# Two-layer cross-attention and Mamba kernel on one core: all five instruction orders rewritten, PSUM banks dealt anew

## The chip, the cores and the metric

The kernel runs on one core of one Trainium2 chip. The metric is the device time of one execution in microseconds. The core has a matrix engine (TensorE, PE in the profile), a vector engine (VectorE, DVE), a scalar engine (ScalarE, ACT), GpSimd (POOL) and a queue that only issues transfers (SyncE, SP). Each engine runs its own instruction list in order and meets the others through semaphores.

## The reference

64 batches of 128 rows and 256 columns (`x`) pass two layers; `ctx` is the other input of both. Cut to its operations:

```python
# layer 0: attention with 16 heads of 16, relu on q, k, v
q = relu(x @ Wq + bq); k = relu(ctx @ Wk + bk); v = relu(ctx @ Wv + bv)
s = where(mask, (q . k) / 4, 1e-9); o = softmax(s) @ v
x = layernorm(o + x) * gamma + beta
# layer 1: a Mamba-2 block, then attention with 8 heads of 32
zxbcdt = rms(x) @ in_proj_w            # z 512, xBC 768, dt 8
xBC = silu(conv4(xBC)); dt = softplus(dt + dt_bias); decay = exp(-dt * exp(A_log))
h = h * decay + (dt * xh) (x) B;  y = h . C + D_skip * xh      # over the 128 rows
x = x + rms(y * silu(z)) @ out_proj_w
q = layernorm(x) @ Wq; k = ctx @ Wk; v = ctx @ Wv
x = x + (softmax((q . k) / sqrt(32)) @ v) @ Wo
```

## The kernel before

The 64 batches go in NG = 32 groups of two; most tiles are 128 x 256 or 128 x 512. A group passes some sixty steps, and each step of each engine is a small Python function of a group `g` and a unit `u` that issues one to some twenty instructions. On TensorE there are, for layer 0, `q`, `k`, `v` (projections), `sA` (scores whose maxima VectorE's `mA` takes), `tn` (the transposed maxima), `sT` (transposed scores, whose exponentials ScalarE's `eA` takes), `av` and `ot`; for the Mamba block `nt`, `cp`, `dp`, `z`, `bd`, `gm`, `bx`, `y`, `o`; for the last attention `ht`, `q1`, `k1`, `v1`, `sC`, `tC`, `oC`, `wp`. A projection is written as three fp32r products of split operands (`proj3`, L328 to L334), whose low parts GpSimd makes (`lo_x` L1842, `lo_c` L1847, `lo_u` L1852). The state recurrence is turned into a 128 x 128 decay matrix per head by `scan` (L1015) on VectorE, from a broadcast through DRAM. GpSimd also has `qm` (the mask on q, L1861), `xr` and `rs` (layer norm of layer 0), `xd`, `dx`, `ga` (the gate, L1931), `yl`, `s2_`, `r2` and `nC` (L1967).

The groups overlap: at any time TensorE works on groups g+2 to g+7. The order of each engine's steps is written out by hand, in five lists: a head, a loop `for g in range(NG - 9)` of 23 iterations whose body holds every step once with different groups, and a tail. Where TensorE has nothing to do in head and tail, the lists hold fillers: `warm(n)` at the start (63 matmuls) and `unread(name, u, g, n)` (190 matmuls), which write to a bank that is about to be overwritten.

PSUM has eight banks. `USES` deals them: an entry `((name, unit, lag), bank)` says which bank a step writes, and the order of the entries is the order of use. `bank()` (L183 to L194) looks up who used the bank before and returns the semaphore at which it is free:

```python
                n, j, lag = order[b][at]
                if 0 <= step - lag < NG:
                    return bank_t[b], freed[n](step - lag, j)
```

So a new dealing makes a step wait for another step's reader. Data waits are in the functions and don't depend on the order. The functions themselves are untouched, but for two waits.

Of the kernel before, what the change touches and what calls it, by code (L numbers as in the profile page):

```python
# [2116 lines left out]
```

## Time and profile before

| | |
|---|---|
| median of 3 runs | 1319.77 us (1319.29 to 1320.99) |
| span of the profiled execution, first to last instruction | 1319.5 us |
| TensorE busy | 1303.4 us, 99% |
| VectorE busy | 1193.6 us, 90% |
| ScalarE busy | 1131.2 us, 86% |
| GpSimd busy | 947.7 us, 72% |

The span is the time of that one execution; it lies 0.3 us under the median. The busy times say how full each engine is on average; whether one of them sets the end is read from the chain that ended last and from what each engine waits for. In the views below, a line such as L332 is a line of the kernel before, a row of a timeline or a chain begins with its start and its length in us, and `<-` in brackets names what ended an engine's idle time.

### The profile page before, as it was taken

The numbers are of one execution on the slowest core, as the hardware profiler recorded it, in microseconds if no ns is written. First come the engines' busy times: TensorE is split into PE (matmuls) and PEld (weight loads), VectorE is DVE, ScalarE is ACT, GpSimd is POOL, SyncE is SP. The second block draws the span as 40 slices with busy tenths as digits, with TensorE's granted clock in tenths as the row PEclk, the third lists the DMA queues.
The fourth block names the chain that finished last, engine by engine and source line by source line (L and its number), as shares of the span: only waits on it lengthen the run. The fifth ranks groups of instructions, "written<-read, shape, count | busy, mean of one in ns | idle before, by whom it ended". The sixth has DMA issues, their size and how long they took to land.

```text
span 1319.5 us, 43916 instructions
## 1 busy us (share of the span) xinstructions
PE 1303.4 (99%) x15877; PEld 1165.5 (88%) x15877; DVE 1193.6 (90%) x3032; ACT 1131.2 (86%) x3407; POOL 947.7 (72%) x1214
## 2 busy tenths in 40 slices
PE   8999999999999999999999999999999999999998
PEld 7888888999888898888998888899888889898887
DVE  6999999999999999999999999999999999999882
ACT  6778888898888898888898888899888899888866
POOL 4777777777777777777677777687777677677674
PEclk9999999999999999999999999999999999999999
DMA  6121122212122212122211122211122222011210
GB/s 208 48 74 50 50 74 78 78 49 67 50 70 78 78 50 66 50 70 78 78 57 59 50 70 78 78 60 57 50 70 78 77 82 62 17 51 58 66 49 25
DMA packets 41285, 87.03 MB, mean 66 GB/s; under 512 B 5744, under 2 KB 10992, under 8 KB 41072
## 3 DMA queue, kind: packets, MB, share of 16 engines
q1 hardware_dynamic: 40560, 83.93, 20.4%
q8 instruction: 129, 2.11, 0.7%
q14 instruction: 84, 0.69, 0.2%
q10 hardware_dynamic: 512, 0.31, 0.1%
HBM read 75.53 MB, written 8.68 MB: 64 GB/s over the span
## 4 chain that ended last, share of the span: by engine, by line
PE 92%; DVE 4%; POOL 2%; issue 1%; DMA 1%; ACT 1%; DVEq 0%; ACTq 0%; POOLq 0%
PE bank L332 28%; PE bank L442 11%; PE bank L573 7%; PE bank L432 5%; PE bank L399 5%; PE bank L456 5%; PE bank L556 5%; PE bank L587 4%; PE bank L692 4%; PE bank L627 3%; PE bank L380 3%; PE bank L648 3%; PE bank L677 2%; PE bank L490 2%; PE bank L436 1%; PE bank L531 1%
## 5 line engine op out<-in xcount | busy, mean ns | idle before, releaser
L991 DVE SCALAR_TENSOR_TENSOR ACC<-bank,cw,ACC 128x250 f32<-128x250 f32 (+2 forms) x576 | 264.5, 462 | 6.4 <-ACT ACC L1561 3.7
L332 PE MATMUL bank<-xnT,wnl 128*128 128x256 f32 x640 | 198.6, 310 | 1.7 <-DVE XC L1004 1.4
L1648 ACT ACTIVATE PC<-bank,stc 128x128 f32<-128x128 f32 x512 | 182.8, 388 | 8.0 <-DVE stc L1103 5.2
L332 PE MATMUL bank<-xnL,wnh 128*128 128x256 f32 x640 | 178.7, 279 | 0.0
L332 PE MATMUL bank<-xnT,wnh 128*128 128x256 f32 x640 | 178.3, 279 | 0.0
L835 DVE TENSOR_REDUCE sta<-bank 128x4 f32<-128x512 f32 x256 | 163.6, 672 | 2.8 <-PE bank L399 2.8
L1015 DVE TENSOR_TENSOR_SCAN L<-DB,id 128x1024 f32<-128x1024 f32 x64 | 146.6, 2290 | 2.2 <-DMA DB<-dec_scratch 2.2
L1967 POOL TENSOR_TENSOR PC<-PC,stc 128x512 f32<-128x512 f32 x128 | 132.4, 1043 | 11.7 <-DVE stc L1110 11.5
L1463 ACT ACTIVATE PTA<-bank 128x512 f32<-128x512 f32 x256 | 133.5, 629 | 6.8 <-PE bank L436 3.9
L332 PEld LDWEIGHTS bank<-xnT,wnl 128*128 128x128 f32 x640 | 120.4, 188 | 21.4 <-issue 16.2
L1922 POOL TENSOR_TENSOR XH<-XH,dtt 128x512 f32<-128x512 f32 x64 | 81.0, 1265 | 56.6 <-ACT XH L1578 56.6
L332 PEld LDWEIGHTS bank<-xnL,wnh 128*128 128x128 f32 x640 | 120.8, 189 | 0.1
L332 PEld LDWEIGHTS bank<-xnT,wnh 128*128 128x128 f32 x640 | 120.1, 188 | 0.0
L1648 ACT ACTIVATION_READ_ACCUMULATOR PC<-bank,stc 128x1 f32 x512 | 116.7, 228 | 0.0
L1847 POOL TENSOR_TENSOR cL<-cT,cH 128x512 fp32r<-128x512 f32 x31 | 59.0, 1903 | 76.8 <-ACT cH L1395 76.8
L1561 ACT ACTIVATE ACC<-bank,cw 128x256 f32<-128x256 f32 x192 | 110.6, 577 | 2.2 <-PE bank L332 1.5
L1931 POOL TENSOR_TENSOR Y<-Y,SZ 128x512 f32<-128x512 f32 x64 | 85.9, 1342 | 18.8 <-DVE Y L1044 16.1
L1937 POOL TENSOR_TENSOR Yl<-Y,Yh 128x512 fp32r<-128x512 f32 x64 | 82.2, 1285 | 17.4 <-ACT Yh L1606 17.4
L1449 ACT ACTIVATE NT<-bank,sel 128x128 fp32r<-128x128 f32 x256 | 73.6, 382 | 21.5 <-PE bank L412 21.5
L1662 ACT ACTIVATE PTC<-bank 128x512 f32<-128x512 f32 x128 | 78.8, 622 | 15.3 <-PE bank L442 15.2
L1103 DVE TENSOR_REDUCE stc<-bank 128x4 f32<-128x512 f32 x128 | 84.3, 681 | 6.9 <-PE bank L652 6.7
L1569 ACT ACTIVATE bank<-ACC 128x256 f32<-128x256 f32 x192 | 79.6, 418 | 11.1 <-DVE ACC L991 10.8
(210 smaller groups left out, 4757.7 us busy)
## 6 DMA issues: line engine op xcount, KB each, us to landing
DB<-dec_scratch SPq DMA_DIRECT2D x64, 512.0 KB, 4.0
cT<-in_cT SPq DMA_DIRECT2D x64, 256.0 KB, 2.7
xt<-in_xt SPq DMA_DIRECT2D x32, 256.0 KB, 3.7
out_x<-X SPq DMA_DIRECT2D x32, 256.0 KB, 4.0
xT<-in_xT SPq DMA_DIRECT2D x31, 256.0 KB, 4.1
QM<-qm_rows SPq DMA_DIRECT2D x31, 128.0 KB, 4.0
XC<-in_win SPq DMA_DIRECT2D x2, 644.0 KB, 6.8
PTC<-in_wout SPq DMA_DIRECT2D x2, 256.0 KB, 4.6
```

What stands on the lines that cost most here:

```text
L332: mm = e.matmul(t[:, c0:c0 + T], wt[:, k, m:m + 128], x[:, k, :], start=(n == 0), stop=(n == 5))
L442: mm = e.transpose(t[:, c0 + i * 128:c0 + (i + 1) * 128], src(i), ident[:, :])
L573: e.matmul(t[:, 0:256], x[:, kk * 128:(kk + 1) * 128], w[:, kk, :], start=(n == 0), stop=(n == 11))
L835: e.tensor_reduce(sta[ns % 4][:, 4 * j:4 * j + 4], t[:, :].rearrange("p (i k) -> p i k", i=4), AX_X, ALU.max, negate=True).then_inc(s_mA, 1)
L991: e.scalar_tensor_tensor(out=w, in0=t[:, 0:T].rearrange("p (b t) -> p b t", b=NB)[:, :, 0:125 + k], scalar=cw[:, c, k:k + 1], in1=w, op0=A ...
L1015: e.tensor_tensor_scan(L[:, :, :].rearrange("p h t -> p (h t)"), DB[b][:, :], id8[:, :, :].rearrange("p h t -> p (h t)"), 0.0, ALU.mult, A ...
L1103: e.tensor_reduce(stc[g % 4][:, 4 * i:4 * i + 4], t[:, :].rearrange("p (i k) -> p i k", i=4), AX_X, ALU.max, negate=True).then_inc(s_mC, 1)
L1463: e.activation(PTA[n % 4][:, :, :], t[:, :].rearrange("p (i k) -> p i k", i=4), ACT.Exp).then_inc(s_eA, 1)
L1561: e.activation(ACC[n % 3][:, :, :], t[:, 0:T].rearrange("p (b t) -> p b t", b=NB), ACT.Identity, bias=cw[:, c, 4:5], scale=cw[:, c, 3:4]). ...
L1648: op = e.activation(PC[n % 4][:, p, :], t[:, p * 128:(p + 1) * 128], ACT.Exp, bias=stc[g % 4][:, 4 * i + p:4 * i + p + 1], accum_out=stc[g ...
L1931: e.tensor_tensor(cv(Y[:, :]), cv(Y[:, :]), SZ[:, :, b * 128:(b + 1) * 128], ALU.mult).then_inc(s_ga, 1)
L1967: e.tensor_tensor(PC[n % 4][:, :, :], PC[n % 4][:, :, :], stc[g % 4][:, 16 + 4 * i:20 + 4 * i].unsqueeze(2).to_broadcast([128, 4, 128]), A ...
```

## The change

The five lists and `USES` are rewritten. Every engine has the same instructions as before (TensorE 11393, VectorE 3032, ScalarE 2834, GpSimd 1210, SyncE 307 issued), and as many fillers. Two waits are added: SyncE waits for the write of the mask rows (`d_qr`) before the weight loads behind `load_c(2)`, and `xs(0, 0)` waits for the small constants (`d_small`). In the loop, TensorE has `v1` before `z`, `tn` of unit 0 before `cp` 2 and `wp`, `tn` of unit 1 before `cp` 5 and `av` instead of after them, `bx` 1 before `v`, and a new order of `gm` 1, `nt` and `tC` 3; the banks of `sT`, `ot`, `sA`, `tn` 1 and `av` 0 are others. In the head, the first scores `sA(0, 0)` come behind `q(1, 0)`, ScalarE's `split_x(1)` before `ke(0, 1)`, GpSimd's `lo_x(1)` before both `qm` of group 0 and `lo_c(2)` behind `xr(0, 1)`, VectorE's `w_hi(0)` behind the maxima of group 0. In the tail the last filler stands before `tC(31, 0)`.

```diff
--- before.py
+++ after.py
 USES = [
-    (("k", 1, 1), 3), (("ot", 0, 2), 5), (("z", 1, 3), 2), (("sT", 4, 2), 1), (("sT", 5, 2), 5), (("sT", 6, 2), 6),
-    (("sT", 7, 2), 0), (("tC", 1, 5), 3), (("k1", 0, 4), 4), (("bx", 0, 3), 7), (("av", 1, 2), 5), (("sA", 0, 1), 4),
+    (("k", 1, 1), 3), (("ot", 0, 2), 0), (("z", 1, 3), 2), (("sT", 4, 2), 1), (("sT", 5, 2), 5), (("sT", 6, 2), 0),
+    (("sT", 7, 2), 6), (("tC", 1, 5), 3), (("k1", 0, 4), 4), (("bx", 0, 3), 7), (("av", 1, 2), 5), (("sA", 0, 1), 4),
     (("sA", 1, 1), 2), (("sA", 2, 1), 1), (("sA", 3, 1), 0), (("ht", 0, 4), 6), (("k1", 1, 4), 3), (("ot", 1, 2), 5),
-    (("q", 0, 0), 7), (("ht", 1, 4), 4), (("q", 1, 0), 3), (("k", 0, 0), 6), (("tC", 2, 5), 2), (("gm", 0, 3), 1),
-    (("q1", 0, 4), 3), (("sA", 4, 1), 4), (("sA", 5, 1), 5), (("sA", 6, 1), 2), (("sA", 7, 1), 7), (("y", 0, 3), 0),
-    (("v", 0, 0), 1), (("bx", 1, 3), 3), (("q1", 1, 4), 6), (("tC", 3, 5), 5), (("nt", 0, 2), 1), (("gm", 1, 3), 0),
+    (("q", 0, 0), 7), (("ht", 1, 4), 4), (("q", 1, 0), 3), (("tC", 2, 5), 2), (("k", 0, 0), 6), (("gm", 0, 3), 1),
...
                     if g == 2:
+                        e.wait_ge(d_qr, 16)
                         for k in range(2):
...
-            load_x(1); load_c(1); load_t(0); load_m(1); load_x(2); load_m(2); load_c(2); load_c(3)
...
+            load_x(1); load_c(1); load_c(2); load_m(1); load_m(2); load_t(0); load_x(2); load_x(3); load_t(1)
...
-            warm(54); q(0, 0); q(0, 1); warm(3); k(0, 0); k(0, 1); warm(6); v(0, 0); sA(0, 0); q(1, 0); q(1, 1); sA(0, 1)
...
+            warm(54); q(0, 0); q(0, 1); k(0, 0); warm(3); warm(6); k(0, 1); v(0, 0); q(1, 0); sA(0, 0); q(1, 1)
+            unread("k", 0, 1, 4); sA(0, 1); tn(0, 0); k(1, 0); unread("sT", 0, 0, 10); sT(0, 0); v(1, 0); av(0, 0)
...
                 q(g + 7, 0)
                 ht(g + 3, 1)
                 q(g + 7, 1)
+                tC(g + 2, 2)
                 k(g + 7, 0)
-                tC(g + 2, 2)
                 gm(g + 4, 0)
                 q1(g + 3, 0)
                 sA(g + 6, 1)
                 y(g + 4, 0)
+                bx(g + 4, 1)
                 v(g + 7, 0)
-                bx(g + 4, 1)
                 q1(g + 3, 1)
+                gm(g + 4, 1)
+                nt(g + 5, 0)
                 tC(g + 2, 3)
-                nt(g + 5, 0)
-                gm(g + 4, 1)
                 sC(g + 3, 0)
                 oC(g + 2, 0)
                 oC(g + 2, 1)
@@ -764,63 +765,63 @@
                 y(g + 4, 1)
                 cp(g + 5, 1)
                 o(g + 4, 0)
+                v1(g + 3, 0)
                 z(g + 5, 0)
-                v1(g + 3, 0)
+                tn(g + 6, 0)
                 cp(g + 5, 2)
                 wp(g + 2, 0)
-                tn(g + 6, 0)
                 cp(g + 5, 3)
                 o(g + 4, 1)
                 sT(g + 6, 0)
                 cp(g + 5, 4)
                 bd(g + 5, 0)
+                tn(g + 6, 1)
                 cp(g + 5, 5)
                 av(g + 6, 0)
                 av(g + 6, 1)
                 av(g + 6, 2)
                 av(g + 6, 3)
-                tn(g + 6, 1)
                 tC(g + 3, 0)
...
+            wp(NG - 2, 0); unread("tC", 3, NG - 1, 6); tC(NG - 1, 0); v1(NG - 1, 0); tC(NG - 1, 1); tC(NG - 1, 2)
+            tC(NG - 1, 3); oC(NG - 1, 0); oC(NG - 1, 1); wp(NG - 1, 0)
...
                     ns = 2 * g + b
+                    if ns == 0:
+                        e.wait_ge(d_small, 16 * 4)
                     e.wait_ge(s_bg, ns + 1)
...
-            w_hi(0)
...
+            w_hi(0); nm(0, 1); nw(0, 1); rc(0, 0); xo(0, 0); bs(0, 0); bg(0, 0); xs(0, 0); x2(0, 0); rc(0, 1)
...
-            split_x(0); split_c(0); qe(0, 0); qe(0, 1); ke(0, 0); ke(0, 1); split_x(1); ve(0, 0); split_c(1)
...
+            split_x(0); split_c(0); qe(0, 0); qe(0, 1); ke(0, 0); split_x(1); ke(0, 1); ve(0, 0); qe(1, 0); split_c(1)
...
-            qm(0, 0); qm(0, 1); lo_x(1); lo_c(1); lo_x(2); qm(1, 0); qm(1, 1); xr(0, 0); lo_c(2); rs(0, 0); xr(0, 1)
...
+            lo_x(1); qm(0, 0); qm(0, 1); lo_c(1); qm(1, 0); lo_x(2); qm(1, 1); xr(0, 0); rs(0, 0); xr(0, 1); lo_c(2)
```

## Rows read from the trace of the kernel before

**Rows 1.** The page, its parts 1 and 4: busy time, and the chain by engine.

```profile
PE 1303.4 (99%) x15877; PEld 1165.5 (88%) x15877; DVE 1193.6 (90%) x3032; ACT 1131.2 (86%) x3407; POOL 947.7 (72%) x1214
...
PE 92%; DVE 4%; POOL 2%; issue 1%; DMA 1%; ACT 1%; DVEq 0%; ACTq 0%; POOLq 0%
```

**Rows 2.** Busy time of each engine in three stretches: head, steady middle, tail.

```profile
0.00:40.00 40.00, 35.54 (x415) 31.31 (x416) 26.72 (x53) 25.60 (x55) 21.53 (x42) 1.00 0.58 187
300.00:616.00 316.00, 316.00 (x3906) 283.31 (x3904) 294.42 (x753) 279.55 (x849) 231.05 (x296) 1.00 0.21 65
1230.00:1319.50 89.50, 80.43 (x867) 70.44 (x865) 56.94 (x138) 61.16 (x197) 55.07 (x66) 1.00 0.16 52
```

**Rows 3.** The chain that ended last: first and last steady L692 (start us, us).

```profile
197.22 1.73 PE bank L692 x8
...
1066.35 1.73 PE bank L692 x8
```

**Rows 4.** Waits of all engines, 300 to 616 us: the largest.

```profile
POOL cL L1847 <- ACT cH L1395: 22.1, 8, 2.8
```

**Rows 5.** Waits of TensorE in the whole run: total, times, longest.

```profile
PE bank L332 <- issue: 2.2, 1, 2.2
```

**Rows 6.** Groups by line and shape, 300 to 616 us: busy, mean ns.

```profile
L1015 DVE TENSOR_TENSOR_SCAN L<-DB,id 128x1024 f32<-128x1024 f32 x16 | 36.5, 2280 | 0.0
...
L1931 POOL TENSOR_TENSOR Y<-Y,SZ 128x512 f32<-128x512 f32 x16 | 20.6, 1286 | 3.4 <-DVE Y L1044 2.6
...
L1847 POOL TENSOR_TENSOR cL<-cT,cH 128x512 fp32r<-128x512 f32 x8 | 15.3, 1915 | 22.1 <-ACT cH L1395 22.1
...
L1852 POOL TENSOR_TENSOR cUl<-cT,cUh 128x512 fp32r<-128x512 f32 x8 | 10.3, 1290 | 0.0
...
L1081 DVE SCALAR_TENSOR_TENSOR stb<-stb 128x1 f32<-128x1 f32 x16 | 9.4, 585 | 0.0
```

**Rows 7.** Timeline of TensorE: start us, us, line, operation.

```profile
619.84 0.60 PE L442 MATMUL bank<-ident,xn 128*128 128x128 f32 x4
620.27 0.39 PE L531 MATMUL bank<-XC 128*128 128x128 f32 x2
...
640.05 0.60 PE L442 MATMUL bank<-ident,PC 128*128 128x128 f32 x4
640.40 0.36 PE L332 MATMUL bank<-cH,wkl 128*128 128x256 f32 x1
640.61 0.28 PE L332 MATMUL bank<-cL,wkh 128*128 128x256 f32 x1
640.72 0.28 PE L332 MATMUL bank<-cH,wkh 128*128 128x256 f32 x1
```

**Rows 8.** Timeline of TensorE and ScalarE around 637 us.

```profile
637.32 2.06 ACT L1463 ACTIVATE PTA<-bank 128x512 f32<-128x512 f32 x4
...
637.97 0.27 PE L501 MATMUL bank<-ident,dts 128*16 128x128 f32 x1
```

**Rows 9.** The chain that ended last, the first 30 us (start us, us).

```profile
6.05 7.00 DMA xT<-in_xT
...
13.62 0.59 ACT V L1439
...
14.25 1.15 PE bank L399 x16
15.39 1.62 PE bank L332 x12
...
18.93 1.15 ACT NT L1449 x4
...
29.25 0.14 DVE keep L1171
29.39 1.23 DVE maskb L1172
```

**Rows 10.** Timeline of GpSimd in the head.

```profile
11.07 2.28 POOL L1861 TENSOR_TENSOR QT<-QT,QM 128x256 f32<-128x256 f32 x2 [1.68 <-DVE QM L1148]
13.79 1.27 POOL L1842 TENSOR_TENSOR xL<-xT,xH 128x512 fp32r<-128x512 f32 x1 [0.44 <-ACT xH L1384]
...
23.26 1.43 POOL L1861 TENSOR_TENSOR QT<-QT,QM 128x256 f32<-128x256 f32 x2
```

**Rows 11.** The chain that ended last, two pieces of the tail.

```profile
1240.21 2.23 issue
...
1278.39 3.12 POOL Y L1931
```

More of the change, by code:

```diff
@@ L1224, in vector @@
+            x2(5, 1); mA(6, 5); yd(4, 0); mA(6, 6); mA(6, 7); scan(4, 1); nl(5, 0); nl(5, 1); mC(3, 0); lg(4, 1)
+            mC(3, 1); d0(5, 0); nw(6, 0); nm(6, 1); mC(3, 2); rC(3, 0); d0(5, 1); tap(5, 0)
             for g in range(NG - 9):
+                yd(g + 4, 1)
                 tap(g + 5, 1)
-                yd(g + 4, 1)
+                mC(g + 3, 3)
                 nw(g + 6, 1)
+                r1(g + 4, 0)
+                tap(g + 5, 2)
                 dc(g + 5, 0)
-                tap(g + 5, 2)
+                tap(g + 5, 3)
@@ L1314, in vector @@
                 d0(g + 6, 0)
-                d0(g + 6, 1)
                 rC(g + 4, 0)
@@ L1728, in scalar @@
                 ve(g + 6, 0)
+                split_x(g + 7)
                 q1e(g + 2, 1)
@@ L1995, in gpsimd @@
-            r2(2, 1); lo_u(2); lo_x(6); hr(2, 0); hr(2, 1); qm(5, 0); qm(5, 1); nC(1, 2); dx(3, 0); xr(4, 0)
-            rs(4, 0); lo_c(6); nC(1, 3); xr(4, 1); xd(3, 0); rs(4, 1); nr(4, 0); nr(4, 1)
+            lo_x(1); qm(0, 0); qm(0, 1); lo_c(1); qm(1, 0); lo_x(2); qm(1, 1); xr(0, 0); rs(0, 0); xr(0, 1); lo_c(2)
+            rs(0, 1); nr(0, 0); nr(0, 1); lo_x(3); qm(2, 0); xr(1, 0); dx(0, 0); rs(1, 0); qm(2, 1); nr(1, 0); lo_c(3)
+            xr(1, 1); xd(0, 0); rs(1, 1); nr(1, 1); ga(0, 0); xd(0, 1); yl(0, 0); dx(0, 1); s2_(0, 0); ga(0, 1)
@@ new lines, in gpsimd @@
+            yl(0, 1); s2_(0, 1); r2(0, 0); lo_u(0); r2(0, 1); lo_x(4); qm(3, 0); qm(3, 1); hr(0, 0); dx(1, 0)
+            xr(2, 0); rs(2, 0); hr(0, 1); lo_c(4); xr(2, 1); nr(2, 0); xd(1, 0); rs(2, 1); nr(2, 1); ga(1, 0)
+            s2_(1, 0); xd(1, 1); yl(1, 0); dx(1, 1); ga(1, 1); yl(1, 1); s2_(1, 1); r2(1, 0); nC(0, 0); r2(1, 1)
+            nC(0, 1); nC(0, 2); qm(4, 0); hr(1, 0); lo_x(5); lo_u(1); xr(3, 0); hr(1, 1); rs(3, 0); qm(4, 1); lo_c(5)
+            dx(2, 0); xd(2, 0); xr(3, 1); nC(0, 3); rs(3, 1); nr(3, 0); nr(3, 1); ga(2, 0); s2_(2, 0); xd(2, 1)
@@ L1997, in gpsimd @@
+            yl(2, 0); dx(2, 1); ga(2, 1); r2(2, 0); s2_(2, 1); yl(2, 1); lo_x(6); qm(5, 0); qm(5, 1); r2(2, 1)
+            nC(1, 0); lo_u(2); hr(2, 0); nC(1, 1); dx(3, 0); xr(4, 0); nC(1, 2); hr(2, 1); rs(4, 0); lo_c(6); nC(1, 3)
+            xr(4, 1); nr(4, 0); xd(3, 0); rs(4, 1); nr(4, 1)
             for g in range(NG - 9):
@@ L1999, in gpsimd @@
                 xd(g + 3, 1)
+                dx(g + 3, 1)
                 s2_(g + 3, 0)
                 yl(g + 3, 0)
-                dx(g + 3, 1)
-                nC(g + 2, 0)
+                lo_x(g + 7)
                 ga(g + 3, 1)
@@ L2006, in gpsimd @@
                 yl(g + 3, 1)
+                qm(g + 6, 0)
                 s2_(g + 3, 1)
+                nC(g + 2, 0)
                 nC(g + 2, 1)
+                r2(g + 3, 1)
                 lo_u(g + 3)
-                qm(g + 6, 0)
-                r2(g + 3, 1)
+                nC(g + 2, 2)
+                hr(g + 3, 0)
                 qm(g + 6, 1)
-                hr(g + 3, 0)
-                lo_x(g + 7)
                 hr(g + 3, 1)
-                nC(g + 2, 2)
+                xr(g + 5, 0)
@@ L2048, in gpsimd @@
-            nC(NG - 2, 3); nC(NG - 1, 0); nC(NG - 1, 1); nC(NG - 1, 2); nC(NG - 1, 3)
+            ga(NG - 6, 0); dx(NG - 6, 1); xd(NG - 6, 1); s2_(NG - 6, 0); yl(NG - 6, 0); ga(NG - 6, 1); nC(NG - 7, 0)
+            r2(NG - 6, 0); qm(NG - 3, 0); yl(NG - 6, 1); s2_(NG - 6, 1); lo_x(NG - 2); r2(NG - 6, 1); qm(NG - 3, 1)
+            lo_u(NG - 6); nC(NG - 7, 1); hr(NG - 6, 0); nC(NG - 7, 2); dx(NG - 5, 0); xr(NG - 4, 0); hr(NG - 6, 1)
+            rs(NG - 4, 0); lo_c(NG - 2); xr(NG - 4, 1); xd(NG - 5, 0); qm(NG - 2, 0); rs(NG - 4, 1); nC(NG - 7, 3)
@@ new lines, in gpsimd @@
+            nr(NG - 4, 0); nr(NG - 4, 1); ga(NG - 5, 0); dx(NG - 5, 1); xd(NG - 5, 1); yl(NG - 5, 0); s2_(NG - 5, 0)
+            ga(NG - 5, 1); r2(NG - 5, 0); yl(NG - 5, 1); s2_(NG - 5, 1); lo_u(NG - 5); r2(NG - 5, 1); lo_x(NG - 1)
+            nC(NG - 6, 0); qm(NG - 2, 1); nC(NG - 6, 1); hr(NG - 5, 0); hr(NG - 5, 1); xr(NG - 3, 0); nC(NG - 6, 2)
+            nC(NG - 6, 3); lo_c(NG - 1); xd(NG - 4, 0); rs(NG - 3, 0); xr(NG - 3, 1); dx(NG - 4, 0); rs(NG - 3, 1)
+            nr(NG - 3, 0); qm(NG - 1, 0); nr(NG - 3, 1); ga(NG - 4, 0); s2_(NG - 4, 0); xd(NG - 4, 1); yl(NG - 4, 0)
```

623 lines of the change are left out of this document (295 added, 328 removed), and 10 rows, old and new, of the table USES.

## The prediction

> **What bounds the kernel now.** I read the page first. TensorE is busy for 1303.4 of the 1319.5 us span, VectorE for 1193.6, ScalarE for 1131.2 and GpSimd for 947.7, and the chain that ended last lies on TensorE for 92% of the span [rows 1]. So the question for every edit is not what it saves on VectorE or GpSimd, but whether TensorE waits for it.
>
> The second view is the busy time by stretch [rows 2]. In 316 us in the middle, TensorE is busy for 316.00 us and VectorE for 294.42. VectorE is at 93%, so it has 21.6 us spare there, and it isn't the bound. The granted clock is 1.00, the 2.4 GHz level, in every stretch. Only the ends have room: TensorE is idle for 40 - 35.54 = 4.46 us in the first 40 us, and for 89.5 - 80.43 = 9.07 us in the last 89.5.
>
> The third view is the chain, where the output projection of every group (L692) is a good clock. It starts at 197.22 and at 1066.35 us with 21 such rows between, so 22 periods take 869.13 us, 39.51 us each [rows 3]. 316 us hold eight periods. The fourth view, the waits of that middle stretch, has no row of TensorE in it; the largest are GpSimd's, 22.1 us for a ScalarE result [rows 4]. The waits of TensorE in the whole run are small: the largest is one of 2.2 us of the kind "issue", in the tail [rows 5]. With all of them at zero, TensorE's 1303.4 us of work would remain.
>
> **The contention, and what relief is worth.** The lines by shape of the middle stretch show GpSimd's subtraction at L1847 (128x512) at 1915 ns, while the one at L1852, of the same shape and output type, takes 1290 [rows 6]. That is 0.63 us once a period; what L1847 meets is VectorE's scan L1015, of 2280 ns. VectorE's L1081, on one number per partition, takes 585 ns twice a period; it can't give back more than all of it, 1.17 us. Together at most 0.63 + 1.17 = 1.8 us a period, some on each engine. In the steady loop it is worth nothing on the path: VectorE gains part of that on 2.7 us (21.6/8) of slack that it already has, and TensorE waits for neither. Its cover is TensorE's own 39.51 us of work; without it the relief would be worth at most 1.8 x 28 = 50 us. I take 0. The Trainium skill ("SBUF — State Buffer", section "SBUF: two separate sides") says that a GpSimd operation and a VectorE operation with two SBUF inputs exclude each other for a whole instruction. The 0.63 us above agree in direction, not in size: full exclusion by a 2.28 us scan could cost more.
>
> **TensorE's order.** The same 11393 instructions are issued, with as many fillers (190 of unread, 63 of warm). What a block costs depends on its neighbour: in the timeline the first matmul of a split projection (fp32r) that follows an fp32 operation starts 0.21 us before the second, which starts 0.11 before the third [rows 7]. The new loop order enters such blocks from fp32 work 16 times a period where the old one does 14 times. Uncompensated, at 0.21 - 0.11 = 0.10 us, that is 0.2 us a period, +5.6 us over 28. But a fp32 block gives most of it back at its end: four transposes followed by fp32 work take 0.43 us (619.84 to 620.27), followed by a split block 0.35 (640.05 to 640.40) [rows 7]. At 0.10 - 0.08 = 0.02 for each of two entries that is +0.04 a period, +1.1 in all. The pairs differ by some hundredths, down to -0.01 a period; I take +0.01, so +0.3 us over 28 periods; bounds -0.3 and +5.6.
>
> **New waits of the loop.** Re-dealing the banks changes what each block waits for. I laid the old times on the new order. The tightest is tn of unit 1, now before cp 5 and in bank 5: it is due at 638.1, behind the transpose L501 of 637.97, and needs the first of ScalarE's four exponentials, which together take 2.06 us from 637.32: a quarter is 0.52, and with what they overlap one ends by some 637.9 [rows 8]. The margin is 0.1 to 0.2 us. The others that I laid out (v1, tn of unit 0, nt, tC 2, the second sT) keep 0.3 to 0.9. Behind a waiting tn stand cp 5, av and the next group's k, and for them VectorE's taps and ScalarE's copies. I take 0; the far bound is a miss of 0.3 us in 25 periods, +7.5.
>
> **The head.** Here a cost is plain. Before, TensorE's first scores (L399) start at 14.25 us. The xT of group 1 takes from 6.05 to 13.05 us to land; ScalarE splits it, copies V from 13.62 on, and the scores follow. The same chain passes q of group 1 at 15.39 and reaches ScalarE's first copy of the transposed maxima (L1449) at 18.93 [rows 9]. In the new order half of q of group 1 stands before the first scores, and GpSimd's lo_x(1) before both qm of group 0. lo_x(1) can't start before ScalarE's split: 13.79, and it ends 1.27 later, at 15.06; then the two qm, 2.28 us at 11.07 beside a busy VectorE, 1.43 for the pair at 23.26 [rows 10]; I take 1.43. The first scores wait for them until 16.5 instead of 14.25, +2.3. Of q's 1.62 us, 0.8 then already lies behind, but the maxima must follow the scores, so L1449 comes about 1.9 us later, near 20.8. Given back: lo_c(2), a GpSimd operation of 1.3 us, no longer meets VectorE's L1172, which took 1.23 us at 29.39, where L1171 on the same mask took 0.14 [rows 9]; of those 1.1 us I take 0.6, since what gates next may be another engine. w_hi(0) moves off the front of VectorE's queue into its idle time. Head +1.3; bounds 0 (later waits take it up) and +2.3. The added wait of load_c(2) on the mask's DMA and of xs(0,0) on small loads lie far after what they wait for, 0; bound +0.5, as SP's queue has later loads behind load_c(2).
>
> **The tail.** The last 60 us are a chain of latencies. In it GpSimd's L1931 takes 3.12 us at 1278.39, against 1.29 in the loop [rows 6, 11]; it starts beside the second scan. The new order keeps ga(31,0) directly beside that scan, and GpSimd's twelve operations behind it stand nearly as before, so the 1.8 us are not recovered. The filler of 6 before the last tC moves ahead of tC(31,0), up to +0.7 us for the first of ScalarE's copies. Mixed otherwise: I take 0, bounds -4 (1.8 for the scan collision and the 2.23 us issue gap at 1240.21 [rows 11], which has no cause in the profile) and +3.
>
> **The sum.** 1319.5 + 0 (contention) + 0.3 (order) + 0 (new waits) + 1.3 (head) + 0 (tail) = 1321.1. The profiled execution's span is 0.3 us under the median of the runs, 1319.77, so I predict 1321.3, rounded to 1321.
>
> **The rivals.**
> 1. Relief reaches the ends. Head and tail hold TensorE idle for 13.5 us [rows 2] and the new orders may shorten these waits: half of the tail's 4, and 2 in the head by earlier nm and mA. For it: L1172 and the 3.12 us of L1931; against it: the 1.9 us computed above. 1321 - 2 - 2 = 1317, to 1315 if all 4 come.
> 2. A bank comes free late in the loop. tn 1 has 0.1 to 0.2 us; from the point where ScalarE's exponential ends 0.2 us later than now, each period pays. 0.1 to 0.3 us x 25 = +2.5 to +7.5: 1324 to 1328. This is the rival on the other side of the first.
> 3. The two extra fp32 entries are not paid back: +5.6, 1326.
> 4. The reordering doesn't reduce the meetings: the steady loop alone decides, and the result is the forecast's, 1320 to 1321. It is inside my forecast.
> 5. VectorE is the true bound, at 93%, and its relief passes on: 1.8 x 28 = 50 us, 1269. No wait of TensorE for VectorE in the middle stretch speaks for it.
> 6. The head's longer gap lowers the clock. TensorE was idle for 4.46 us in the first 40 at 1.00 [rows 2]; one gap there grows by 2.3. No row shows the lower level, so I can only say that work done at 1.2 GHz takes twice as long: above 1325.
>
> **How the numbers follow.** Within 0.2%, 2.6 us, a measurement can't tell a change of this kernel from none, so faster is under 1317.1 and slower above 1322.4. Chances: forecast (1319 to 1323, rival 4 in it) 0.52, of which 0.40 is within the bound and 0.12 just above; rival 1 0.22; rival 2 0.13; rival 3 0.07; rival 5 0.02; rival 6 0.01; the tail alone worse by up to 3 us 0.03. Faster is 0.24 (rivals 1 and 5), slower 0.36 (0.12 + 0.13 + 0.07 + 0.01 + 0.03), the rest 0.40. The range 1315 to 1328 leaves out rivals 5 and 6 and the far ends of 1 and 2, under 0.2. The forecast's own range is 1319 to 1323.
>
> **What would show it.** The L692 rows should stay 39.5 us apart (39.4 to 39.6), with no TensorE row in the waits of the middle stretch; a wait of tn (L412) or L332 for ScalarE's L1463 there is rival 2, a longer period without a wait is rival 3, a shorter one breaks the forecast. L1847 and L1081 should come near 1290 and 200 ns if the meetings go. The first scores should start near 16.5 us, L1449 near 20.8, and the L692 row that stood at 197.22 should come 1 to 2 us later. L1931 should still show about 3 us once in the tail. The prediction is wrong if the first scores start as before, or if the distance from the last steady L692 row to the end changes by over 3 us.

## The result, and the profile after

The changed kernel takes 1330.46 us (median of 4 runs, 1329.92 to 1334.52), the kernel before 1319.59 in the runs beside it: ratio 1.0081, 95% interval 1.006 to 1.0102. It is 11 us slower. The prediction said 1321, with 1315 to 1328 for 8 times in 10; the result lies outside. The profiled execution of the changed kernel is its longest, 1334.52 us with a span (first to last instruction) of 1332.7. In the runs that list both, a time lies about 1.8 us above its span, so a usual execution spans 1328.7. The line numbers of the changed kernel are 1 to 5 off those of before: L332 is now L333, L692 is L693, L1081 is L1084.

The page of the changed kernel, parts 1 and 4, to be read beside [rows 1]:

```profile
PE 1307.4 (98%) x15877; PEld 1170.1 (88%) x15877; DVE 1203.2 (90%) x3032; ACT 1128.9 (85%) x3407; POOL 947.2 (71%) x1214
...
PE 89%; DVE 3%; ACT 2%; DMA 2%; POOL 2%; issue 2%; SPq 1%; ACTq 0%; POOLq 0%; DVEq 0%
```

TensorE is busy for only 4 us more, but the span is 13 longer, and in the chain "SPq" (SyncE issuing) is new, at 1%, and DMA has gone from 1% to 2%. The busy time by stretch, beside [rows 2] (columns: length, busy of TensorE, its weight loads, VectorE, ScalarE, GpSimd, granted clock, DMA share, GB/s):

```profile
0.00:40.00 40.00, 28.21 (x312) 24.87 (x313) 17.21 (x39) 19.07 (x40) 12.20 (x32) 0.96 0.52 170
28.00:32.00 4.00, 0.00 (x0) 0.00 (x0) 0.00 (x0) 1.58 (x4) 0.87 (x1) 0.98 0.29 98
32.00:36.00 4.00, 3.92 (x45) 3.44 (x46) 0.00 (x0) 2.92 (x9) 1.36 (x3) 0.59 0.29 70
120.00:125.00 5.00, 4.81 (x50) 3.98 (x49) 2.34 (x4) 2.99 (x12) 3.97 (x5) 0.56 0.01 3
125.00:130.00 5.00, 5.00 (x30) 4.45 (x31) 3.75 (x12) 3.11 (x17) 0.60 (x2) 0.50 0.00 0
300.00:616.00 316.00, 315.98 (x3939) 284.53 (x3939) 298.57 (x758) 279.55 (x851) 232.07 (x299) 1.00 0.20 65
```

The first 40 us hold 28.21 us of TensorE work where they held 35.54. From 28 to 32 TensorE does nothing, and from 32 to 36 it is granted 0.59 of its clock; from 120 to 130 us 0.56 and 0.50, the 1.2 GHz level, behind a second wait. The middle looks as before. The chain, beside [rows 3]:

```profile
214.15 1.73 PE bank L693 x8
...
1079.40 1.73 PE bank L693 x8
```

Again 22 periods, but in 865.25 us: 39.33 each, 0.18 less than before. So the loop became faster, by 4 us in all, and the head much slower: the L693 that answers to the row of 197.22 stands at 214.15, 16.9 us later. Some 5 of these belong to this one execution. The run tn1_late (below) has the same head, and its trace has no second fall of the clock:

```profile
16.00:20.00 4.00, 3.59 (x25) 2.68 (x24) 1.08 (x2) 0.99 (x2) 1.93 (x2) 0.55 0.04 12
...
120.00:125.00 5.00, 5.00 (x74) 4.37 (x75) 4.38 (x10) 4.14 (x20) 3.71 (x4) 1.00 0.01 3
```

Its clock fell earlier, from 16.4 to 23.2 us. From 115 to 127 us it gains 5.3 us on the trace of the changed kernel, and its row stands at 208.5, 11.5 us later than before. So the clock falls at different places in different executions of the same head, and what the head costs in a usual one is nearer 12 us than 17.

**Where the head loses.** The waits of TensorE in the whole run, beside [rows 5], and the chain from 25.9 us on:

```profile
PE bank L457 <- ACT PTA L1462: 5.5, 2, 5.3
PE bank L376 <- DVE vbias L1148: 2.0, 1, 2.0
PE bank L443 <- ACT V L1438: 2.0, 1, 2.0
```

```profile
22.62 0.43 SPq L281
...
25.94 4.46 DMA xT<-in_xT
...
30.42 0.63 ACT xH L1383
31.05 0.98 ACT PTA L1462 x2
...
32.08 1.94 PE bank L457 x32
```

Read from the bottom: TensorE's av (L457) waits 5.3 us for ScalarE's first exponential, which stands in ScalarE's queue behind the split of xT(2) (L1383), which waits for a transfer that SyncE issues at 25.94 us. SyncE's queue shows why it is so late; first the changed kernel, then the kernel before:

```profile
11.79 0.50 SPq L246 DMA_DIRECT2D qm_rows<-Q1T  x1
18.52 0.33 SPq L243 DMA_DIRECT2D cT<-in_cT  x1
18.90 0.91 SPq L250 DMA_DIRECT2D PTC<-in_wout  x2
...
22.62 0.90 SPq L281 DMA_DIRECT2D QM<-qm_rows  x2
...
25.94 6.81 SPq L236 DMA_DIRECT2D xT<-in_xT  x2
```

```profile
15.08 0.33 SPq L236 DMA_DIRECT2D xT<-in_xT  x1
...
16.32 0.69 SPq L243 DMA_DIRECT2D cT<-in_cT  x1
```

In the new list `load_c(2)` (L243) stands in front of `load_x(2)` (L236). It can't be issued before GpSimd's lo_c(1) is done, at 18.5 us, and behind it come thirteen transfers (weights, mask rows, the rows of `xt`, constants), 0.47 us from one issue to the next, but 1.34 us behind one of them. xT(2) is issued 10.9 us later than before.

**What the meetings of VectorE and GpSimd did.** The groups by line and shape of the same stretch, beside [rows 6]; the second fence has the lines of before that rose:

```profile
L1018 DVE TENSOR_TENSOR_SCAN L<-DB,id 128x1024 f32<-128x1024 f32 x16 | 38.4, 2400 | 0.0
...
L1890 POOL TENSOR_TENSOR sta<-sta,mhalf 128x1 f32<-128x1 f32 x16 | 11.0, 689 | 1.3
...
L1842 POOL TENSOR_TENSOR cL<-cT,cH 128x512 fp32r<-128x512 f32 x8 | 10.9, 1367 | 24.7 <-ACT cH L1394 24.7
...
L855 DVE TENSOR_TENSOR NM<-sta,NM 128x16 fp32r<-128x16 f32 x16 | 8.1, 505 | 0.0
...
L1888 POOL TENSOR_SCALAR sta<-sta 128x1 f32<-128x1 f32 x16 | 5.9, 367 | 0.0
...
L1084 DVE SCALAR_TENSOR_TENSOR stb<-stb 128x1 f32<-128x1 f32 x16 | 1.8, 151 | 0.0
```

```profile
L1895 POOL TENSOR_TENSOR sta<-sta,mhalf 128x1 f32<-128x1 f32 x16 | 9.0, 562 | 1.3
...
L1893 POOL TENSOR_SCALAR sta<-sta 128x1 f32<-128x1 f32 x16 | 3.5, 218 | 1.9 <-DVE sta L891 1.3
...
L854 DVE TENSOR_TENSOR NM<-sta,NM 128x16 fp32r<-128x16 f32 x16 | 2.7, 167 | 0.0
```

L1081 fell from 585 to 151 ns and GpSimd's L1847 by half a microsecond. But L854 rose from 167 to 505 ns, the scan by 0.12 us, L1893 and L1895 by 0.15 and 0.13 each. Over 19 whole periods of the middle GpSimd is busy for 28.9 us a period in both kernels, VectorE for 37.2 us where it was 36.8. The meetings were moved, not removed, and VectorE has more to carry than before; the loop became faster all the same.

### The profile page after: what moved, and what is told of

The parts are those of the page before. It is cut to its first block, busy times and chain, and to the rows that moved or that the text cites. A ratio compares the mean times of both kernels' runs of the same rounds, so it can differ in the third digit from the quotient of the medians.

```text
span 1332.7 us, 43917 instructions
## 1 busy us (share of the span) xinstructions
PE 1307.4 (98%) x15877; PEld 1170.1 (88%) x15877; DVE 1203.2 (90%) x3032; ACT 1128.9 (85%) x3407; POOL 947.2 (71%) x1214
## 4 chain that ended last, share of the span: by engine, by line
PE 89%; DVE 3%; ACT 2%; DMA 2%; POOL 2%; issue 2%; SPq 1%; ACTq 0%; POOLq 0%; DVEq 0%
PE bank L333 26%; PE bank L443 11%; PE bank L574 6%; PE bank L433 5%; PE bank L557 5%; PE bank L400 5%; PE bank L457 5%; PE bank L588 4%; PE bank L693 4%; PE bank L628 3%; PE bank L381 3%; PE bank L649 3%; PE bank L678 2%; PE bank L491 2%; PE bank L532 1%
## 5 line engine op out<-in xcount | busy, mean ns | idle before, releaser
L994 DVE SCALAR_TENSOR_TENSOR ACC<-bank,cw,ACC 128x250 f32<-128x250 f32 (+2 forms) x576 | 268.0, 470 | 14.5 <-ACT ACC L1560 5.6
L333 PE MATMUL bank<-xnT,wnl 128*128 128x256 f32 x640 | 202.6, 317 | 1.2 <-DVE XC L1007 1.1
L836 DVE TENSOR_REDUCE sta<-bank 128x4 f32<-128x512 f32 x256 | 164.7, 675 | 16.5 <-PE bank L400 16.4
L333 PE MATMUL bank<-xnL,wnh 128*128 128x256 f32 x640 | 179.0, 280 | 0.0
L333 PE MATMUL bank<-xnT,wnh 128*128 128x256 f32 x640 | 178.8, 279 | 0.0
L1018 DVE TENSOR_TENSOR_SCAN L<-DB,id 128x1024 f32<-128x1024 f32 x64 | 152.8, 2388 | 0.0
L1462 ACT ACTIVATE PTA<-bank 128x512 f32<-128x512 f32 x256 | 133.5, 623 | 15.0 <-PE bank L437 14.7
L333 PEld LDWEIGHTS bank<-xnT,wnl 128*128 128x128 f32 x640 | 121.1, 189 | 19.3 <-issue 16.2
L1560 ACT ACTIVATE ACC<-bank,cw 128x256 f32<-128x256 f32 x192 | 111.7, 583 | 18.5 <-PE bank L333 18.3
L333 PEld LDWEIGHTS bank<-xnL,wnh 128*128 128x128 f32 x640 | 121.4, 190 | 0.7
L333 PEld LDWEIGHTS bank<-xnT,wnh 128*128 128x128 f32 x640 | 120.7, 189 | 0.0
L1842 POOL TENSOR_TENSOR cL<-cT,cH 128x512 fp32r<-128x512 f32 x31 | 43.6, 1405 | 86.5 <-ACT cH L1394 86.5
L1007 DVE SCALAR_TENSOR_TENSOR XC<-bank,ACC 128x256 f32<-128x256 f32 x192 | 80.2, 418 | 18.6 <-ACT bank L1568 17.9
L1932 POOL TENSOR_TENSOR Yl<-Y,Yh 128x512 fp32r<-128x512 f32 x64 | 83.3, 1301 | 14.3 <-ACT Yh L1605 14.2
```

What stands on the lines that cost most here:

```text
L333: mm = e.matmul(t[:, c0:c0 + T], wt[:, k, m:m + 128], x[:, k, :], start=(n == 0), stop=(n == 5))
L836: e.tensor_reduce(sta[ns % 4][:, 4 * j:4 * j + 4], t[:, :].rearrange("p (i k) -> p i k", i=4), AX_X, ALU.max, negate=True).then_inc(s_mA, 1)
L994: e.scalar_tensor_tensor(out=w, in0=t[:, 0:T].rearrange("p (b t) -> p b t", b=NB)[:, :, 0:125 + k], scalar=cw[:, c, k:k + 1], in1=w, op0=A ...
L1018: e.tensor_tensor_scan(L[:, :, :].rearrange("p h t -> p (h t)"), DB[b][:, :], id8[:, :, :].rearrange("p h t -> p (h t)"), 0.0, ALU.mult, A ...
L1462: e.activation(PTA[n % 4][:, :, :], t[:, :].rearrange("p (i k) -> p i k", i=4), ACT.Exp).then_inc(s_eA, 1)
L1560: e.activation(ACC[n % 3][:, :, :], t[:, 0:T].rearrange("p (b t) -> p b t", b=NB), ACT.Identity, bias=cw[:, c, 4:5], scale=cw[:, c, 3:4]). ...
```

## The experiments

Each kernel was timed in five rounds beside the kernel before, but for sp_old2, which was run once.

**1 and 2: SyncE's head order.** First its whole old head list put back (`sp_old`), then one call moved (`sp_x2`):

```diff
-            load_x(1); load_c(1); load_c(2); load_m(1); load_m(2); load_t(0); load_x(2); load_x(3); load_t(1)
+            load_x(1); load_c(1); load_x(2); load_c(2); load_m(1); load_m(2); load_t(0); load_x(3); load_t(1)
```

> The changed kernel with SyncE's head list of before; all else as changed. Theory S (SyncE's queue): in the changed kernel the load of xT(2) stands behind load_c(2), whose own wait ends at 18.5 us, and behind eleven further transfers, so it is issued at 25.94 instead of 15.08 us; ScalarE and then TensorE wait for it, 5.3 us once, and the load of xT(5) behind load_t(3) costs 2.0 us at 118; the clock falls behind both. With the old list both waits and both falls go: the first L693 comes at 159 us instead of 173.3, and since the steady period of 39.30 us stays, the time is 1316 (1314 to 1318), faster than before. Rival H (the head orders of TensorE, ScalarE and GpSimd do it): the first L693 stays over 170 us and the time is 1328 or more.

> The changed kernel with load_x(2) alone moved in front of load_c(2) in SyncE's list. Theory S: xT(2) is issued before 17 us, the wait of 5.3 us and the clock's fall at 32 to 36 us go, the wait of 2.0 us at 118 (xT(5) behind load_t(3)) stays or shrinks: 1320 to 1323. If one queue position explains all, 1316. Rival H: 1328 or more.

Measured: sp_old 1334.72 us (1333.67 to 1334.76 without one execution of 3073.58 us, which is left out), sp_x2 1323.62 us. One call moved gives 6.8 us back, as theory S said (6.1 if each kernel is taken against the kernel before in its own rounds, 1319.59 and 1318.89); the whole old list gives nothing. So theory S was right about xT(2), and wrong in that the old list would do. It was run once more for its trace:

> The kernel of sp_old once more, for a trace of an ordinary execution. The old list of SyncE alone did not help (1334.7 us). Theory S2: SyncE's order and GpSimd's must fit each other; GpSimd's lo_c(2) now stands behind xr(0,1), and the old list has load_c(3), which waits for lo_c(2), in front of load_x(3) and load_t(1), so xT(3) comes 8 us or more later than before and ScalarE and TensorE wait for it. Time 1332 to 1336. Rival: xT(2) still lands late, for another reason.

Measured: 1336.34 us. Its waits of TensorE, and SyncE's queue:

```profile
PE bank L532 <- DVE sta L836: 6.8, 1, 6.8
```

```profile
15.91 0.43 SPq L236 DMA_DIRECT2D xT<-in_xT  x1
...
21.44 0.43 SPq L253 DMA_DIRECT2D wo<-in_wo  x1
42.41 0.33 SPq L243 DMA_DIRECT2D cT<-in_cT  x1
42.78 0.43 SPq L281 DMA_DIRECT2D QM<-qm_rows  x1
43.26 0.43 SPq L236 DMA_DIRECT2D xT<-in_xT  x1
...
67.23 0.33 SPq L281 DMA_DIRECT2D QM<-qm_rows  x1
67.60 0.43 SPq L287 DMA_DIRECT2D dec_scratch<-decT  x1
```

xT(2) is issued at 15.91 again. Now SyncE stands from 21.9 to 42.4 us at `load_c(3)`, which waits for the lo_c(2) that the change had moved behind xr(0,1) on GpSimd, and from 49.5 to 67.2 at `load_m(4)`, which waits for a qm that GpSimd's new order also has later; the decay matrices of group 0 (`dec_out`, 67.60) go out behind it, and TensorE waits 6.8 us. Theory S2's form holds, but the block that it named is the small one. Against sp_x2, TensorE falls 1.0 us behind at 50 us, where xT(3) comes late, and 9.1 between 70 and 77 us, at the second block, with the clock low from 74.4 to 84.6 us. SyncE's list is neither good nor bad by itself, it must fit GpSimd's.

**3: the new SyncE list on the kernel before.** Its head list and the wait for `d_qr` alone.

> The kernel before with SyncE's new head list and its new wait for the mask rows; all else as before. Theory S: it loses what the changed kernel loses in its head, 10 to 16 us: 1330 to 1335, with xT(2) issued after 23 us. Rival H: within 3 us of before, 1318 to 1322.

Measured: 1327.39 us, 8.5 us above before (1318.89 in these runs). That is less than the 10 to 16 expected, and far from the rival's 1322: xT(2) is issued at 23.69, TensorE waits 5.2 us once, and the first L692 is 8.5 us late.

**4: the start of the other lists (`x2_start`).** The prediction's own step on the head, on top of sp_x2:

```diff
-            warm(54); q(0, 0); q(0, 1); k(0, 0); warm(3); warm(6); k(0, 1); v(0, 0); q(1, 0); sA(0, 0); q(1, 1)
+            warm(54); q(0, 0); q(0, 1); k(0, 0); warm(3); warm(6); k(0, 1); v(0, 0); sA(0, 0); q(1, 0); q(1, 1)
...
-            split_x(0); split_c(0); qe(0, 0); qe(0, 1); ke(0, 0); split_x(1); ke(0, 1); ve(0, 0); qe(1, 0); split_c(1)
+            split_x(0); split_c(0); qe(0, 0); qe(0, 1); ke(0, 0); ke(0, 1); split_x(1); ve(0, 0); split_c(1); qe(1, 0)
...
-            lo_x(1); qm(0, 0); qm(0, 1); lo_c(1); qm(1, 0); lo_x(2); qm(1, 1); xr(0, 0); rs(0, 0); xr(0, 1); lo_c(2)
+            qm(0, 0); qm(0, 1); lo_x(1); lo_c(1); qm(1, 0); lo_x(2); qm(1, 1); xr(0, 0); rs(0, 0); xr(0, 1); lo_c(2)
```

> The kernel of sp_x2 (1323.6 us) with the first scores back in front of q(1,0), ScalarE's ke(0,1) in front of split_x(1), and GpSimd's two qm of group 0 in front of lo_x(1). By the prediction's step on the head this order cost 1.9 us up to L1449: the first scores go back from 16.5 to 17.4 us to 14.3 to 15.2, and the time falls by 1.5 to 2.5 us, to 1321 to 1322. Rival: later waits of the head take it up: 1323 to 1324.

Measured: 1320.85 us, 2.8 less than sp_x2. The first scores start at 14.2 us, in the changed kernel at 16.5. A part of the 2.8 may be the clock's: in the trace of sp_x2 it is low from 13.0 to 19.8 us, in that of x2_start not. Among the executions whose mean clock is given as 1.000 the difference is 2.2.

**5: the second late transfer (`x2s_x5`).** On top of x2_start:

```diff
-            dec_in(1, 0); load_c(4); load_t(3); dec_in(1, 1); load_m(4); load_x(5); load_u(1); dec_out(2); load_m(5)
+            dec_in(1, 0); load_c(4); load_m(4); load_x(5); load_t(3); dec_in(1, 1); load_u(1); dec_out(2); load_m(5)
```

> The kernel of x2_start (1320.85 us) with load_m(4) and load_x(5) of SyncE's head list in front of load_t(3) and dec_in(1,1). Theory S: in x2_start the load of xT(5) is issued at 102.8 us, behind load_t(3), and TensorE waits 1.1 us for ScalarE's V behind split_x(5); blocks after it are 1.3 us later than those before it. With the load earlier that step goes: 1319.5 us (1319.0 to 1320.0), as fast as before within 0.1%. Rival: the wait has another cause (buffer or GpSimd's low part), and the time stays at 1320.5 to 1321.

Measured: 1320.09 us, 0.8 less. xT(5) is issued at 94.9 instead of 102.8 us. Laid beside the trace of x2_start, TensorE gains 1.35 us between 107 and 113 us, where the wait was. The later L693 rows don't show it, since this trace had lost 1.7 us near 65 us, in a wait for ScalarE (L1471) that lies ahead of the moved calls. So the transfer is worth some 1.3 us in the trace; the medians show 0.8. The interval (0.9996 to 1.0014) doesn't tell this kernel from the kernel before.

**6 and 7: the clock in the wait.** Fillers in front of av(0,0), first into av's own bank, then into one that is free.

```diff
-sT(0, 0); v(1, 0); av(0, 0)
+sT(0, 0); v(1, 0); unread("q", 0, 2, 38); av(0, 0)
```

after_fill has `unread("av", 0, 0, 38)` there.

> The changed kernel with 38 fillers of 0.118 us on TensorE (4.5 us) in front of av(0,0), in the place of its wait of 5.3 us. Theory C: the wait also costs clock (granted 0.59 from 32 to 36 us in the profiled execution, 4 x 0.41 = 1.6 us); with TensorE busy through it the clock stays at 1.00 there and the time falls by 1 to 2 us, to 1328.5 to 1329.5. Rival: the work behind the wait is bound by other engines, which hide the slower TensorE, and the time stays at 1330 to 1331.

> The changed kernel with 38 fillers of 0.118 us on TensorE in front of av(0,0), this time into a bank that is free by then (that of q(2,0)), so that they lie in the wait of 5.3 us. Theory C: the wait also costs clock; with TensorE busy through it the granted clock stays at 1.00 from 28 to 40 us and the time falls by 1 to 2 us against the changed kernel's 1330.5, to 1328.5 to 1329.5. Rival: other engines hide the slower TensorE there, and the time stays at 1330 to 1331.

Measured: after_fill 1335.09 us. It tells nothing of the clock: av's bank is itself freed by ScalarE's exponentials, so the fillers waited too and ran behind the wait. In its trace they wait 3.2 us for ScalarE (L1462), and then take 6.3 us at a low clock. after_fill2: 1328.80 us, 1.7 less than the changed kernel. Its stretches:

```profile
28.00:32.00 4.00, 3.27 (x28) 3.07 (x26) 0.00 (x0) 1.19 (x3) 0.48 (x1) 1.00 0.24 80
32.00:36.00 4.00, 3.48 (x49) 2.69 (x49) 0.63 (x3) 3.45 (x10) 1.74 (x3) 1.00 0.21 66
```

With TensorE busy through the wait the clock stays at 1.00 there. Three of its five executions have a mean clock of 1.000; none of the eight of the changed kernel and of tn1_late has, they show 0.995 to 0.999. That 4.5 us of added work cost nothing is clear. The 1.7 us gained are less sure: against the kernel before, the ratios are 1.0068 (1.0054 to 1.0083) and 1.0081 (1.006 to 1.0102), and the trace of after_fill2 gains 0.8 us behind group 23, far from the fillers. The clock at 120 us is 1.00 here too, but so it is in tn1_late, which has no fillers.

**8 and 9: which edit made the loop shorter.** By blocks of TensorE (mean start to start, 300 to 1015 us), the saving per period lies in two: the second half of av went from 1132 to 1011 ns, z of unit 1 from 1587 to 1544. In the second each of the twelve products starts 114 instead of 118 ns after the one before it. The rest are pairs that cancel, as predicted: v1 +84 and z -80, wp -187 with cp 2 +77 and cp 3 +108, gm -95 and tC 3 +96.

The first edit is in TensorE's loop of the changed kernel, the second (`before_actloop`) takes ScalarE's whole new loop list into the kernel before:

```diff
-                tn(g + 6, 1)
                 cp(g + 5, 5)
                 av(g + 6, 0)
                 av(g + 6, 1)
                 av(g + 6, 2)
                 av(g + 6, 3)
+                tn(g + 6, 1)
```

> The changed kernel with tn of unit 1 put back behind the four av in the loop, its bank (5) as changed. Theory T: the steady period fell from 39.51 to 39.30 us because the earlier tn lets ScalarE's L1448 (nt_) end earlier, so that its four exponentials (L1462) no longer come late for the last weight loads of av (L457); with tn back, the period is 39.43 to 39.50 and the time 3 to 4.6 us above the changed kernel's, 1333.5 to 1335. Rival B (the other swaps, or the order of blocks itself): the period stays at 39.30 and the time at 1330.5.

> The kernel before with ScalarE's new loop order alone (no bank, no other list is changed). Theory A: four exponentials (L1463) reach av's last weight loads (L456) 0.12 us late each period because ScalarE's own queue is backlogged there by 0.16 us; the new order, with pC behind the second nt_, takes that away: the block of av 4 to 7 goes from 1132 to 1011 ns, the period to 39.38 to 39.40 and the time down by 2.5 to 3.5 us. Rival B: the saving needs tn or the banks too; the period stays at 39.48 to 39.51 and the time within 1 us of before.

Measured: tn1_late 1330.44 us, period 39.37: z 1 is back at 1591 ns, av stays at 1011. So tn's place is worth 0.04 us a period, by z and not by av, and the theory as put falls. Why it makes z shorter isn't shown. before_actloop 1363.28 us: ScalarE's new loop order on the old others costs 1.9 us a period (41.40). 1.2 of these are a wait of TensorE at L693:

```profile
PE bank L693 <- DVE X L1064: 26.3, 22, 1.2
```

It can't tell what av waits for. A narrower edit, in x2_start:

```diff
+                pC(g + 2, 0)
                 nt_(g + 5, 1)
-                pC(g + 2, 0)
```

> The kernel of x2_start with ScalarE's pC(g+2,0) back in front of nt_(g+5,1) in the loop, as before. Theory A: this swap is what brought the four exponentials forward by 0.16 us; the block of av 4 to 7 goes from 1011 back to some 1110 to 1130 ns, the period from 39.32 to 39.43 us, the time up by 2 to 3 us to 1323 to 1324. Rival B (the gain is from what leads up to it on VectorE or TensorE, as tn's earlier place): the period stays within 0.03 us and the time at 1320.5 to 1321.5.

Measured: 1320.40 us, period 39.34, av at 1011. Not that either.

**10 and 11: one VectorE operation.** The weight loads of av in the middle of before wait for ScalarE's exponentials (the first fence, the waits of TensorE's weight loads); the second fence is VectorE's timeline there, 0.46 us a tap (L991) with L1081 between two of them:

```profile
PEld bank L456 <- ACT PTA L1463: 1.7, 9, 0.3
PEld bank L442 <- ACT KT L1427: 1.7, 7, 0.2
```

```profile
638.55 0.46 DVE L991 SCALAR_TENSOR_TENSOR ACC<-bank,cw,ACC 128x252 f32<-128x252 f32 x1
638.94 0.70 DVE L1081 SCALAR_TENSOR_TENSOR stb<-stb 128x1 f32<-128x1 f32 x1
639.56 0.47 DVE L991 SCALAR_TENSOR_TENSOR ACC<-bank,cw,ACC 128x254 f32<-128x254 f32 x1
```

```diff
-                hm(g + 4, 0)
                 tap(g + 5, 11)
...
                 xo(g + 6, 0)
+                hm(g + 4, 0)
                 hm(g + 4, 1)
                 tap(g + 5, 16)
```

> The kernel before with one edit: VectorE's hm(g+4,0) (L1081) stands behind xo(g+6,0) instead of between tap 10 and tap 11 in the loop. Theory V: at its old place it takes 0.7 us for one number per partition, beside GpSimd; tap 11 and with it ScalarE's L1569, L1472 and four exponentials come 0.16 us late, and the last weight loads of av wait 0.12 us each period. With hm moved, the block of av 4 to 7 goes from 1132 to 1011 ns, the period from 39.51 to 39.39, the time to 1316.3 (1315.5 to 1317). Rival: ScalarE's own load sets it; the period stays at 39.48 to 39.51 and the time at 1318.5 to 1319.5.

> The control: the kernel before with VectorE's hm(g+4,1) moved, from behind xo(g+6,0) to behind kk1(g+4,0), and hm(g+4,0) left where it was. Theory V: the late tap is the one behind hm(g+4,0), so nothing is won: av 4 to 7 at 1110 to 1135 ns, period 39.48 to 39.51, time 1318.5 to 1319.5. Rival (less contention anywhere helps): 1316 to 1317.5.

Measured: before_hm0 1316.60 us against 1319.22 (ratio 0.998, interval 0.997 to 0.999); the control, with hm(g+4,1) moved instead, 1319.13. Its rows:

```profile
L1081 DVE SCALAR_TENSOR_TENSOR stb<-stb 128x1 f32<-128x1 f32 x16 | 1.7, 150 | 0.0
```

```profile
PEld bank L456 <- ACT PTA L1463: 0.3, 1, 0.3
```

```profile
197.20 1.73 PE bank L692 x8
...
1064.12 1.73 PE bank L692 x8
```

L1081 takes 150 ns, the wait of the weight loads fell from 1.7 to 0.3 us in eight periods, av is at 1011 ns, and 22 periods take 866.92 us, 39.41 each. In the control L1081 fell too, to 425 ns on average, but the one in front of tap 11 stayed long (0.70 us), and so did av's wait (1.6 us). So this one operation in front of tap 11 is the cause of av's wait. Alone it would be 0.15 us long; whether it would hold av up at that length, with no GpSimd operation beside it, was not tested. The way between, tap 11, ScalarE's L1569 and L1472 and then the exponentials, is read from the timelines, where each of these stands 0.1 to 0.35 us earlier against sT in the kernels with the short av.

**12: do the parts add?** The new dealing, tn early and hm moved, heads and tails of before.

> The kernel before with the new PSUM dealing, tn(g+6,1) in front of cp 5 and av in TensorE's loop, and hm(g+4,0) moved as in before_hm0; heads, tails and all other orders as before. If the loop's saving is made of av (0.12 us, hm) and z 1 (0.05 us, tn), each period is 39.32 to 39.36 and the time 1315 to 1316, faster than both kernels by over 0.2%. If the parts don't add: 1316.5 to 1319.

Measured: 1316.52 us (ratio 0.9975, interval 0.9965 to 0.9986), period 39.37. It is the fastest kernel of the study, beside before_hm0. av and z are both short, but the new dealing gives 0.03 of a period, not 0.05 to 0.09 more. And what the loop gained is lost behind it: from the output projection of group 23 to that of group 31 its trace takes 247.6 us, that of before_hm0 245.4.

**13 and 14: head and tail by themselves.** The old heads of all lists before the new loop and tail (`head_old`), and the old tails behind x2_start.

> The heads of all five lists of before, the loops, tails and PSUM dealing of the changed kernel. Theory: the change has two parts of opposite sign: the head costs some 15 us, the loop returns 0.20 us a period. With the old heads the first L693 stands at 157 to 158 us as before, the period is 39.30 to 39.32, and the time 4 to 5 us below before: 1314 to 1316. Rival: the loop's shorter period depends on how the new head leaves the queues (the phase between the engines), and goes with it: period 39.5, time 1318 to 1321.

> The kernel of x2_start (1320.85 us) with the tails of all five lists of before. In the trace of before, 248.15 us pass from the L692 row of group 23 to that of group 31, but 2.3 of them are one gap of the kind issue at 1240 us that no later trace of an old tail shows (before_hm1 has 246.29); the new tails take 248.1 to 248.4. Theory E: the new tail costs 2 us, and with the old one the time is 1318.4 to 1319.2. Rival: the gap is chance and the tails are equal (the prediction's 0): 1320.5 to 1321.2.

Measured: head_old 1320.52 us, not 1315. The period is 39.33, so the loop's gain doesn't depend on the head; but the seam costs 2.7 us once (groups 1 to 2), and the rest is in the tail. x2s_oldtail 1327.33 us: its seam costs 7.4 us in two groups against x2_start, so its time tells nothing of the tail. Beyond the seam, from the output projection of group 25 to that of group 31, it takes 0.8 us less than x2_start. That lists of different versions can be joined doesn't make the joint free.

## Why the prediction was wrong

**The wait that was costed at nothing.** The step reads: "The added wait of load_c(2) on the mask's DMA and of xs(0,0) on small loads lie far after what they wait for, 0; bound +0.5, as SP's queue has later loads behind load_c(2)." It failed, and it is most of the miss. The wait on `d_qr` is free, as said: the row at 11.79 lands before 18.5. But load_c(2) has a wait of its own, for lo_c(1), and it was moved in front of load_x(2) with thirteen transfers between the two. The step named the queue behind it and didn't follow it to the engine that waits. Measured: 6.8 us (sp_x2), of which up to 1.7 are the clock's (after_fill2). The new order of the head fed it: lo_c(1) ends at 18.5 us instead of 16.3, 1.4 later since both qm of group 0 now stand between lo_x(1) and it, and 0.8 later since ScalarE's `split_c(1)` now stands behind `qe(1, 0)`.

**The rest of the head.** The mechanism was right: the first scores start at 16.5 us, as predicted, by the same three moves, and L1448 (the predicted 20.8) at 21.2. The term was 1.3 us net of 0.6 given back, and measured 2.2 to 2.8 (x2_start). The 0.6 isn't there: lo_c(2) now stands between xr(0,1) and rs(0,1) in the chain of sp_x2, where it costs its own 1.24 us. In x2_start the L693 row that answers to the one at 197.22 is still 2.6 us late: 1.3 are the second late transfer, which the prediction didn't have, and 1.3 stay open.

**The loop.** Predicted 0.3 us slower; measured 3.9 us faster over the 22 periods (3.4 against the trace of before_hm1, whose loop runs as before's). The cost by neighbours was right, its pairs cancel as said. What failed is "In the steady loop it is worth nothing on the path ... TensorE waits for neither". The view of waits has rows for TensorE's matmuls and for its weight loads, and only the first was read: [rows 4] is from that answer, and two lines in it, L456 for ScalarE's exponentials and L442 for KT, 1.7 us each in eight periods, showed a hidden wait of 0.4 us a period. A TensorE busy for 316.00 of 316 us was read as waiting for nothing; a busy matmul can be one whose weights come late. Rival 5 was right in that relief on VectorE can reach TensorE, by the 0.12 us a period by which one chain was late, and wrong in that VectorE is the bound: it is busy for 0.4 us more a period, and the loop is shorter.

**The meeting.** "Full exclusion by a 2.28 us scan could cost more", the prediction says, and takes the 0.63 us as agreeing in direction only. The trace of before has both:

```profile
607.52 2.28 DVE L1015 TENSOR_TENSOR_SCAN L<-DB,id 128x1024 f32<-128x1024 f32 x1
608.98 1.92 POOL L1847 TENSOR_TENSOR cL<-cT,cH 128x512 fp32r<-128x512 f32 x1 [2.77 <-ACT cH L1395]
```

GpSimd's operation starts when most of the scan is over. In the 23 such meetings between 200 and 1100 us it ends 1.08 to 1.10 us after the scan's end; in the changed kernel, where it starts 0.31 us before that end and not 0.87, again 1.08 to 1.09. What a meeting costs is the rest of the first operation, not the whole of it.

**New waits, tail, rivals.** No bank came free late in the loop; rivals 2 and 3 didn't happen. Rival 6 did, with up to 1.7 us in the median, but as a follower of the queue. The tail was put at 0 (-4 to +3). From the L692 of group 23 to that of group 31 the new tail takes 247.5 to 248.4 us in the ten traces that have it; the old one takes 248.15 in the trace of before, but 2.3 of these are the issue gap of [rows 11], which TensorE doesn't have in any later trace of an old tail (245.4 to 246.3 in before_hm0, before_hm1 and before_spnew). So the new tail costs about 2 us. Whether its lists do is not shown: before_best has the old lists with the new dealing of the banks, and takes 247.6. The run that should have shown it failed at its seam. That same gap makes the profiled execution of before a long one: by the 1.8 us of the other runs its span of 1319.5 means a time of about 1321.3, so the note that it lies 0.3 us under the median compared a span with times.

Of the signs that the prediction named, the first scores, L1847 (1367 ns), L1081 (151 ns) and the 3.12 us of the old L1931 once in the tail came as said. The period of 39.33 us and the L692 row, 11 us late and not 1 to 2, broke it.

**The sum again:** SyncE's queue 6.8, start 2.8, second transfer 1.3, rest of the head 1.3, tail 2, loop -3.9 to -3.4: 10.3 to 10.8 of 10.9 us. The terms come from rounds and traces taken at different times, in which the kernel before itself differs by 0.9 us, so a sum this close is partly luck.
